# Turned copies of the slots' logits, two separate powers, and later inverses in a decoder block

## The chip, the cores and the metric

The kernel runs on one core of a Trainium2 chip. The metric is the time of one execution on the device in microseconds. Before the change the median of three runs is 528.75 us (527.16 to 528.95).

A core has several engines with instruction queues of their own, which wait for one another by semaphores: TensorE (PE in the profile, its weight loads PEld), VectorE (DVE), ScalarE (ACT), GpSimd (POOL), and SyncE (SP), which issues the DMAs here.

## The reference, cut to what matters

Self-attention, then cross-attention over 64 sequences, then a soft mixture of experts. The change lies in the last part. N is 64 tokens, D 128, 16 experts with 16 slots each (256 slots), and S 128 sequences.

```python
xn = _layernorm(x, ln_gamma, ln_beta)
x_unit = _l2norm(xn, axis=-1)                 # x / max(norm, 1e-12)
mu_unit = _l2norm(mu, axis=0)
logits = jnp.einsum('bnd,des->bnes', x_unit * scale, mu_unit)
dispatch = jax.nn.softmax(logits, axis=1)     # over the tokens
combine = jax.nn.softmax(logits.reshape(B, N, E * S), axis=-1)   # over the slots
slot_in = jnp.einsum('bnd,bnes->besd', xn, dispatch)
h = gelu(jnp.einsum('besd,edh->besh', slot_in, w1) + b1)
slot_out = jnp.einsum('besh,ehd->besd', h, w2) + b2
out = jnp.einsum('besd,bnes->bnd', slot_out, combine)
x = x + out
```

The same logits are wanted twice: with tokens on the partitions (for `dispatch` and its use as a weight), and with slots on the partitions (for `combine`).

## The kernel before

The work is cut into 16 chunks of 512 tokens (8 sequences). Three stages follow each other: self-attention (to about 130 us), cross-attention (to about 300 us), and the experts, in two halves. The first half, called dispatch here (class `Dispatch`, about 300 to 446 us), computes norms, logits, both softmaxes' exponentials, the slots' inputs and the hidden layer before its GELU; the second, combine (class `SecondLayer`, to the end), does GELU, the second matmul, and the sum over slots.

In dispatch all engines walk over steps t = -1 to 15, one chunk a step, in an order that is written out by hand, and each engine works on another chunk: at step t DVE takes the statistics of chunk t+5 (`moments`, `gathered`), the sums of squares of t+3 (`total`), the unit tokens of t+2 (`unit`), and the maxima of t+1 (`maxima`, `negate`). PE at step t computes the slots' logits of chunk t+1 (`logits_T`: 2 matmuls of 512 columns), half of the slots' inputs of chunk t (`gather`), the tokens' logits of t+1 (`logits`: 4 matmuls of 256 columns from the turned unit tokens `xuT` and `mu`), the other half of `gather`, then turns the maxima (`turn_maxima`), turns the unit tokens of t+2 (`turn_tokens`), adds the negated maxima to both sets of logits (`shifts`), and does the first expert layer and the softmax sums of chunk t (L1424, L1432). ACT does the layernorm's scaling (`hat_of`), the squares, the copies out of PSUM and the exponentials. POOL at step t multiplies chunk t+3 with gamma and adds beta (`affine`), scales the hidden layer of chunk t-3 with the inverse softmax sums (L1303), adds the bias (L1307), and computes `roots`: (variance + eps)^-0.5 of chunk t+5 and the inverse norm of chunk t+3 in one power of 8 columns.

The softmax sums travel by DMA: SP sends them to memory (`send_sums`), fetches them in another layout (`fetch_sums`), DVE inverts them (`invert`, tile e_inv), SP sends the inverses (`inverses_out`) and fetches them spread over partitions (`inverses_in`, tile e_rden). All of it stands in SP's queue, one after the other. The last two inverses are sent in `tail_sp` in the first steps of combine; DVE inverts chunk 14 after its last work of dispatch, and chunk 15 after step 2 of combine.

## Time and profile before

| | value |
|---|---|
| median of 3 runs | 528.75 us |
| the profiled execution | 530.01 us |
| its span on the core | 528.1 us |
| PE busy | 479.7 us, 91% |
| DVE busy | 401.5 us, 76% |
| ACT busy | 366.6 us, 69% |
| POOL busy | 291.9 us, 55% |
| granted TensorE clock, mean | 0.989 |

The span lies inside the time of the execution; 1.9 us are around it. A row of a timeline has the start, the length, the engine, the line, the operation, the tiles (out<-in), and in brackets how long the engine was idle before it and what released it. Rows that follow each other on PE overlap a little, since the next matmul enters while the last one drains; the distance of two starts is what the work takes in sequence.

### The profile page before, as it was taken

How to read it: one execution, taken by the hardware profiler on the slowest of the kernel's cores; microseconds unless marked ns; L12 is line 12 of the kernel's file. 1: busy time of each engine (PE TensorE's matmuls, PEld its weight loads, DVE VectorE, ACT ScalarE, POOL GpSimd, SP SyncE). 2: the span in 40 equal slices, each digit the busy share in tenths (PEclk: the TensorE clock that was granted, in tenths of full speed). 3: DMA queues.
4: the chain of work that ended last, by engine and by line, in shares of the span. 5: the costliest groups of instructions: out<-in, count | busy, mean ns of one | idle time of the engine just before them, and what ended most of it. 6: DMA issues, size and time to landing. Idle time of an engine off the chain costs nothing. (4 is left out here: it accounts for less than half of the span.)

```text
span 528.1 us, 21715 instructions
## 1 busy us (share of the span) xinstructions
PE 479.7 (91%) x8732; PEld 325.9 (62%) x8732; DVE 401.5 (76%) x1095; ACT 366.6 (69%) x554; POOL 291.9 (55%) x398
## 2 busy tenths in 40 slices
PE   3999978989779999999997889999999997889996
PEld 2777756655346666666665645656565655668885
DVE  4788568889998898998978666666666544669896
ACT  3888735556678888787887568887889667445550
POOL 4444133555677868787757747798889731111000
PEclk9999989999999999999999989999999999899999
DMA  5377447540000101101111012232322224256554
GB/s 189 87 182 207 121 134 186 145 135 0 3 24 26 44 25 37 35 26 43 26 46 44 3 41 83 83 104 84 107 82 105 83 104 148 80 159 198 187 182 137
DMA packets 53313, 49.32 MB, mean 93 GB/s; under 512 B 14064, under 2 KB 40944, under 8 KB 53232
## 3 DMA queue, kind: packets, MB, share of 16 engines
q1 hardware_dynamic: 53232, 48.20, 30.6%
q8 instruction: 56, 0.92, 0.7%
q14 instruction: 25, 0.20, 0.1%
HBM read 30.87 MB, written 17.04 MB: 91 GB/s over the span
## 5 line engine op out<-in xcount | busy, mean ns | idle before, releaser
L613 DVE TENSOR_REDUCE c_mx<-ps 128x16 f32<-128x1024 f32 x64 | 77.9, 1218 | 12.2 <-PE ps L795 12.1
L553 POOL TENSOR_TENSOR copies_or_layer<-k_or_hidden,w_mask 128x512 bf16<-128x512 f32 x80 | 83.6, 1071 | 1.2 <-DVE c_work L644 1.2
L714 ACT ACTIVATE c_work<-ps 128x2048 f32<-128x2048 f32 x32 | 60.0, 1874 | 27.3 <-PE ps L824 27.3
L1474 ACT ACTIVATE copies_or_layer<-k_or_hidden 32x512 f32 (+1 forms) x64 | 40.2, 628 | 30.9 <-PE ps L1502 30.3
L1349 ACT ACTIVATE e_slot_in<-ps 128x1024 f32<-128x1024 f32 x30 | 30.6, 1019 | 26.0 <-PE ps L1404 26.0
L1303 POOL TENSOR_TENSOR e_scaled<-e_raw,e_rden 128x512 f32<-128x512 f32 x16 | 20.8, 1300 | 45.2 <-DMA e_rden<-dispatch_inverses 45.2
L1487 DVE TENSOR_TENSOR o_slot_out<-ps,w_b 128x512 f32<-128x512 f32 x64 | 40.9, 682 | 5.9 <-PE ps L1502 5.3
L724 ACT ACTIVATE c_q_bd<-x_all,w_mask 128x512 f32<-128x512 f32 x64 | 42.7, 715 | 0.0
L1579 PE MATMUL ps<-o_slot_out,ctx_sb 128*64 128x129 f32 x512 | 37.6, 286 | 4.1 <-DVE o_slot_out L1487 3.7
L1502 PE MATMUL ps<-w_w,copies_or_layer 64*32 64x128 f32 x2048 | 38.1, 277 | 1.2 <-DVE o_slot_out L1487 0.6
L573 POOL COPY c_v_bd<-v_or_front 64x512 f32<-64x512 f32 x32 | 21.8, 682 | 29.8 <-PE ps L844 28.7
L1404 PE MATMUL ps<-copies_or_layer,v_or_front 64*128 64x256 f32 x256 | 36.6, 406 | 0.4 <-ACT copies_or_layer L1371 0.4
L824 PE MATMUL ps<-c_q_bd,k_or_hidden 32*64 32x256 f32 x1024 | 35.7, 375 | 0.9 <-issue 0.9
L1579 PEld LDWEIGHTS ps<-o_slot_out,ctx_sb 128*64 128x64 f32 x512 | 29.9, 139 | 10.4 <-issue 9.8
L844 PE MATMUL ps<-c_work,c_v_bd 128*18 128x64 f32 x2048 | 34.9, 220 | 0.1
L1404 PEld LDWEIGHTS ps<-copies_or_layer,v_or_front 64*128 64x128 f32 x256 | 22.5, 189 | 19.6 <-issue 17.1
L844 PEld LDWEIGHTS ps<-c_work,c_v_bd 128*18 128x18 f32 x2048 | 29.4, 98 | 7.5 <-issue 7.5
L1149 PE MATMUL ps<-v_or_front,w_mu 128*128 128x512 f32 x64 | 32.8, 636 | 1.3 <-ACT v_or_front L1366 1.3
L1502 PEld LDWEIGHTS ps<-w_w,copies_or_layer 64*32 64x32 f32 x2048 | 29.3, 107 | 7.5 <-issue 7.2
L795 PE MATMUL ps<-copies_or_layer,c_q_lead 64*64 64x512 bf16 x256 | 26.4, 399 | 6.5 <-DVE c_mx L613 3.8
L1159 PE MATMUL ps<-w_mu,v_or_front 128*128 128x256 f32 x128 | 31.8, 391 | 0.0
L1262 DVE RECIPROCAL e_inv<-e_sums 128x16 f32<-128x16 f32 x16 | 4.0, 253 | 35.9 <-DMA e_sums<-dispatch_sums 35.9
...
## 6 DMA issues: line engine op xcount, KB each, us to landing
...
```

The source lines that it names most:

```text
L553: ins = nc.gpsimd.tensor_tensor(k_bd[:, c.m2, s, :], k32[:, c.v, :], w["mask8"][:, s:s + 1].to_broadcast([P, TOK]), ALU.mult)
L613: nc.vector.reduce_max(mx[:, c.m2, :, p], ps[:, SCORE:SCORE + 2, :].rearrange("p a (h m) -> p (a h) m", m=N), AX_X).then_inc(mx_sb.sem, 1)
L714: nc.scalar.activation(prob[:, h, :], ps[:, 0:4, :].rearrange("p a b -> p (a b)"), ACT.Exp, scale=float(HD) ** -0.5).then_inc(p_sb.sem, 1)
L724: ins = nc.scalar.activation(q_bd[:, c.m2, j, :], q32[:, c.v, :], ACT.Copy, scale=w["mask4"][:, j:j + 1])
L824: ins = nc.tensor.matmul(ps[N * r:N * (r + 1), T, a * 4 * N:(a + 1) * 4 * N].rearrange("p (j n) -> p j n", j=4), k32[rows, c.v, k_at:k_at ...
L844: ins = nc.tensor.matmul(ps[32 * j:32 * j + 2 * V1, VALUE, to:to + N], v_bd[:, c.m2, 2 * a + u, 4 * T + j, :], prob[:, u, of:of + N], star ...
L1149: ins = self.nc.tensor.matmul(self.ps[:, 3 + h, :], self.w["mu"][:, h * P:(h + 1) * P], self.xuT[:, c.m2, :], start=True, stop=False, skip ...
L1404: ins = nc.tensor.matmul(ps[:, bank + r, a * ES:(a + 1) * ES], xn[at, c.m4, 2 * h + a, :], disp[at, c.m2, 2 * h + a, :], start=True, stop= ...
L1474: ins = self.nc.scalar.activation(self.h_bd[at, c.m2, :, :, e % 2, :].rearrange("p s g k -> p g s k"), self.hidden[at, :, bass.ts(c.v, SC ...
L1487: self.nc.vector.tensor_tensor(self.slot_out[:, c.m2, 4 * u:4 * u + 4, a, 0:D], self.ps[:, 2 * u + a, :].rearrange("p (s d) -> p s d", s=4 ...
L1502: ins = self.nc.tensor.matmul(self.ps[32 * q:32 * (q + 1), 2 * u + a, i * D:(i + 1) * D], self.h_bd[rows:rows + 64, c.m2, (i % 2) * PC + 2 ...
L1579: ins = nc.tensor.matmul(ps[N * r:N * (r + 1), 4 + h, (p % 2) * (D + 1):(p % 2 + 1) * (D + 1)], comb[:, c.m2, a, s * N:(s + 1) * N], slot_ ...
```

## The change

In `logits` PE no longer multiplies the unit tokens with `mu`; DVE copies the slots' logits out of PSUM into a new tile `lT` (`copies`: 2 copies of 512 columns a step), and PE turns that copy, with 8 transposes of 128 columns. The turned unit tokens are copied out of PSUM by DVE (`turned_by_dve`) instead of ACT. On POOL the three small operations of the variance become one, and the power of 8 columns becomes two of 4 (`roots` for chunk t+5, `norms` for chunk t+3), and the bias stands behind them. In DVE's step the statistics stand ahead of `unit`, and `invert` stands between the copies and the maxima, one step later than before. SP sends the sums ahead of the inverses of the chunk before. The inverses of chunks 13, 14 and 15 are sent in six steps of combine instead of two in four, and DVE inverts chunk 14 after step 0 and chunk 15 after step 3 of combine.

```diff
@@ cross_attention, POOL @@
-                dispatch.roots(pool, Chunk(None, 0), None)
-                dispatch.roots(pool, Chunk(None, 1), None)
+                dispatch.roots(pool, Chunk(None, 0))
+                dispatch.roots(pool, Chunk(None, 1))
                 dispatch.affine(pool, Chunk(None, 0))
                 dispatch.affine(pool, Chunk(None, 1))
-                dispatch.roots(pool, Chunk(None, 2), Chunk(None, 0))
-                dispatch.roots(pool, Chunk(None, 3), Chunk(None, 1))
+                dispatch.roots(pool, Chunk(None, 2))
+                dispatch.norms(pool, Chunk(None, 0))
+                dispatch.roots(pool, Chunk(None, 3))
+                dispatch.norms(pool, Chunk(None, 1))
@@ Dispatch @@
-    def roots(self, pool, c, u):
-
-        nc, w, root = self.nc, self.w, self.root
-        both, mv = self.inv_root, self.mv
-        if c:
-            pool.wait_ge(self.stat.sem, self.stat.at(c))
-            if c.plus(-2): pool.wait_ge(self.hat_sb.sem, self.hat_sb.at(c.plus(-2)))
-            v, rc = mv[:, c.m2, :, 1], both[:, c.m2, 1]
-            nc.gpsimd.tensor_tensor(rc, v, w["ln_eps"][:], ALU.add).then_inc(root.sem, 1)
-            pool.wait_ge(root.sem, root.at(c, 1))
-            nc.gpsimd.tensor_tensor(rc, rc, w["ln_eps"][:], ALU.mult).then_inc(root.sem, 1)
-            pool.wait_ge(root.sem, root.at(c, 2))
-            nc.gpsimd.tensor_tensor(rc, rc, v, ALU.add).then_inc(root.sem, 1)
-            pool.wait_ge(root.sem, root.at(c, 3))
-        if u: pool.wait_ge(self.clamped.sem, self.clamped.at(u))
-        if c and u:
-            nc.gpsimd.tensor_tensor(both[:, c.m2], both[:, c.m2], self.halves[:], ALU.pow).then_inc(root.sem, 1)
-            pool.wait_ge(root.sem, root.at(c, 4))
-        elif c:
-            nc.gpsimd.tensor_tensor(both[:, c.m2, 1], both[:, c.m2, 1], self.halves[:, 1], ALU.pow).then_inc(root.sem, 1)
-            pool.wait_ge(root.sem, root.at(c, 4))
-        elif u:
-            nc.gpsimd.tensor_tensor(both[:, u.m2, 0], both[:, u.m2, 0], self.halves[:, 0], ALU.pow).then_inc(self.last_unit, 1)
-        if c:
-            nc.gpsimd.tensor_tensor(self.shift[:, c.m2], mv[:, c.m2, :, 0], both[:, c.m2, 1], ALU.mult).then_inc(root.sem, 1)
-            pool.wait_ge(root.sem, root.at(c, 5))
-            nc.gpsimd.tensor_tensor(self.shift[:, c.m2], self.shift[:, c.m2], self.minus[:], ALU.mult).then_inc(root.sem, 1)
+    def roots(self, pool, c):
+        if not c:
+            return
+        nc, root, mv, rc, shift = self.nc, self.root, self.mv, self.inv_root[:, c.m2, 1], self.shift[:, c.m2]
+        pool.wait_ge(self.stat.sem, self.stat.at(c))
+        if c.plus(-2): pool.wait_ge(self.hat_sb.sem, self.hat_sb.at(c.plus(-2)))
+        nc.gpsimd.tensor_scalar(rc, mv[:, c.m2, :, 1], 1.0 + LN_EPS, LN_EPS ** 2, ALU.mult, ALU.add).then_inc(root.sem, 1)
+        pool.wait_ge(root.sem, root.at(c, 1))
+        nc.gpsimd.tensor_tensor(rc, rc, self.halves[:], ALU.pow).then_inc(root.sem, 1)
+        pool.wait_ge(root.sem, root.at(c, 2))
+        nc.gpsimd.tensor_tensor(shift, mv[:, c.m2, :, 0], rc, ALU.mult).then_inc(root.sem, 1)
+        pool.wait_ge(root.sem, root.at(c, 3))
+        nc.gpsimd.tensor_tensor(shift, shift, self.minus[:], ALU.mult).then_inc(root.sem, 1)
+
+    def norms(self, pool, c):
+        if not c:
+            return
+        pool.wait_ge(self.clamped.sem, self.clamped.at(c))
+        self.nc.gpsimd.tensor_tensor(self.inv_root[:, c.m2, 0], self.inv_root[:, c.m2, 0], self.halves[:], ALU.pow).then_inc(self.inverse.sem, 1)
...
-        if c.plus(2): dve.wait_ge(self.root.sem, self.root.at(c.plus(2), 4))
-        else: dve.wait_ge(self.last_unit, c.v - (CHUNKS - 2) + 1)
+        dve.wait_ge(self.inverse.sem, self.inverse.at(c))
...
+    def copies(self, dve, c):
+        if not c:
+            return
+        if c.plus(-1): dve.wait_ge(self.lA_ps.sem, self.lA_ps.at(c.plus(-1)))
+        for h in range(2):
+            dve.wait_ge(self.lT_ps.sem, self.lT_ps.at(c, h + 1))
+            self.nc.vector.tensor_copy(self.lT[:, h, :], self.ps[:, 3 + h, :]).then_inc(self.lT_sb.sem, 1)
+
+    def turned_by_dve(self, dve, c):
+        if not c:
+            return
+        dve.wait_ge(self.xuT_ps.sem, self.xuT_ps.at(c))
+        if c.plus(-2): dve.wait_ge(self.lT_ps.sem, self.lT_ps.at(c.plus(-2)))
+        self.nc.vector.tensor_copy(self.xuT[:, c.m2], self.ps[:, 0, :]).then_inc(self.xuT_sb.sem, 1)
@@ Dispatch.logits_T, logits @@
-        ins.then_inc(self.lT_ps.sem, 1)
+            ins.then_inc(self.lT_ps.sem, 1)
...
+        pe.wait_ge(self.lT_sb.sem, self.lT_sb.at(c))
         for p in range(PC):
-
-            ins = self.nc.tensor.matmul(self.ps[:, 1 + p // 2, p % 2 * ES:(p % 2 + 1) * ES], self.xuT[:, c.m2, p * P:(p + 1) * P],
-                                        self.w["mu"][:], start=p % 2 == 0, stop=False, skip_group_check=True)
+            for h in range(2):
+
+                at = p % 2 * ES + h * P
+                ins = self.nc.tensor.matmul(self.ps[:, 1 + p // 2, at:at + P], self.lT[:, h, p * P:(p + 1) * P], self.w["ident"][:],
+                                            start=p % 2 == 0 and h == 0, stop=False, is_transpose=True, skip_group_check=True)
@@ Dispatch.rest @@
             if k == 0:
-                inverses_out(sp, end.plus(-1))
+                inverses_out(sp, end.plus(-2))
                 send_sums(sp, end)
             elif k == 1:
-                inverses_in(sp, end.plus(-1))
+                inverses_in(sp, end.plus(-2))
                 fetch_sums(sp, end)
             elif k == 2:
+                inverses_out(sp, end.plus(-1))
+            elif k == 3:
+                inverses_in(sp, end.plus(-1))
+            elif k == 4:
...
+                c = t.plus(0)
+                if c and c.plus(1): send_sums(sp, c)
                 c = t.plus(-1)
-                if c and c.plus(2):
+                if c and c.plus(3):
                     inverses_out(sp, c)
                     inverses_in(sp, c)
                 c = t.plus(0)
-                if c and c.plus(1):
-                    send_sums(sp, c)
-                    fetch_sums(sp, c)
+                if c and c.plus(1): fetch_sums(sp, c)
...
+                self.roots(pool, t.plus(5))
+                self.norms(pool, t.plus(3))
+                if c:
                     pool.wait_ge(divided.sem, divided.at(c))
                     nc.gpsimd.tensor_tensor(hidden[:, :, c.v * QS:(c.v + 1) * QS], scaled[:, c.m2],
                                             w["b1"][:].rearrange("p (g o) -> p g o", o=1).to_broadcast([P, 4, QS]),
                                             ALU.add).then_inc(biased.sem, 1)
-                self.roots(pool, t.plus(5), t.plus(3))
...
+                    self.moments(dve, t.plus(5))
                     self.unit(dve, t.plus(2))
-                    self.moments(dve, t.plus(5))
+                    self.copies(dve, t.plus(1))
+                    c = t.plus(-2)
+                    if c and c.plus(3): invert(dve, c)
                     self.maxima(dve, t.plus(1))
                     self.gathered(dve, t.plus(5))
                     self.negate(dve, t.plus(1))
                 self.total(dve, t.plus(3))
-                c = t.plus(-1)
-                if c and c.plus(2): invert(dve, c)
+                self.turned_by_dve(dve, t.plus(2))
...
-            invert(dve, end.plus(-1))
+            invert(dve, end.plus(-2))
...
-                self.turned(act, t.plus(2))
@@ SecondLayer.rest, DVE @@
-                if t.i is None and t.k == 2: dispatch.invert(dve, Chunk(None, CHUNKS - 1))
+                if t.i is None and t.k == 0: dispatch.invert(dve, Chunk(None, CHUNKS - 2))
+                if t.i is None and t.k == 3: dispatch.invert(dve, Chunk(None, CHUNKS - 1))
```

One step of DVE's queue in the middle of dispatch, before (e_stats statistics, e_cm and e_rm maxima, e_ss sums of squares, L1092 the unit tokens):

```order
L1092 TENSOR_TENSOR v_or_front<-v_or_front,e_inv_root 128x512
L1051 BN_STATS e_stats<-x_all 128x6 x4
L1101 TENSOR_REDUCE e_cm<-ps 128x16
L1105 TENSOR_REDUCE e_rm<-ps 128x2 x2
L1062 BN_AGGR e_mv<-e_stats 128x2 x4
L1113 TENSOR_SCALAR e_neg<-ps 128x256
L1081 TENSOR_REDUCE e_ss<-v_or_front 128x4
L1084 TENSOR_SCALAR e_inv_root<-e_ss 128x4
L1262 RECIPROCAL e_inv<-e_sums 128x16
```

The same step after:

```order
L1049 BN_STATS e_stats<-x_all 128x6 x4
L1089 TENSOR_TENSOR v_or_front<-v_or_front,e_inv_root 128x512
L1098 COPY e_lT<-ps 128x512 x2
L1281 RECIPROCAL e_inv<-e_sums 128x16
L1113 TENSOR_REDUCE e_cm<-ps 128x16
L1117 TENSOR_REDUCE e_rm<-ps 128x2 x2
L1060 BN_AGGR e_mv<-e_stats 128x2 x4
L1125 TENSOR_SCALAR e_neg<-ps 128x256
L1079 TENSOR_REDUCE e_ss<-v_or_front 128x4
L1082 TENSOR_SCALAR e_inv_root<-e_ss 128x4
L1105 COPY v_or_front<-ps 128x512
```

Three copies out of PSUM are added (L1098 twice, L1105), the statistics stand ahead of the unit tokens, and the inverse of the sums stands behind the copies.

One step of POOL's queue in the middle of dispatch, before (e_halves is the power of -0.5, w_gamma and w_beta the affine part, L1303 and L1307 the hidden layer of an earlier chunk):

```order
L1009 TENSOR_TENSOR e_inv_root<-e_mv,w_ln_eps 128x4
L1011 TENSOR_TENSOR e_inv_root<-e_inv_root,w_ln_eps 128x4
L1013 TENSOR_TENSOR e_inv_root<-e_inv_root,e_mv 128x4
L1017 TENSOR_TENSOR e_inv_root<-e_inv_root,e_halves 128x8
L1025 TENSOR_TENSOR e_shift<-e_mv,e_inv_root 128x4
L1027 TENSOR_TENSOR e_shift<-e_shift,e_minus 128x4
L997 TENSOR_TENSOR v_or_front<-v_or_front,w_gamma 128x512
L999 TENSOR_TENSOR v_or_front<-v_or_front,w_beta 128x512
L1303 TENSOR_TENSOR e_scaled<-e_raw,e_rden 128x512
L1307 TENSOR_TENSOR k_or_hidden<-e_scaled,w_b 128x4x128
```

The same step after:

```order
L1001 TENSOR_TENSOR v_or_front<-v_or_front,w_gamma 128x512
L1003 TENSOR_TENSOR v_or_front<-v_or_front,w_beta 128x512
L1322 TENSOR_TENSOR e_scaled<-e_raw,e_rden 128x512
L1013 TENSOR_SCALAR e_inv_root<-e_mv 128x4
L1015 TENSOR_TENSOR e_inv_root<-e_inv_root,e_halves 128x4
L1017 TENSOR_TENSOR e_shift<-e_mv,e_inv_root 128x4
L1019 TENSOR_TENSOR e_shift<-e_shift,e_minus 128x4
L1025 TENSOR_TENSOR e_inv_root<-e_inv_root,e_halves 128x4
L1329 TENSOR_TENSOR k_or_hidden<-e_scaled,w_b 128x4x128
```

The bias of the hidden layer (L1329) now stands right behind the power that gives the inverse norms (L1025).

DVE's queue from the last maxima of dispatch into combine, before (L1335 the last slots' inputs, o_slot_out the second layer's output with its bias):

```order
L1105 TENSOR_REDUCE e_rm<-ps 128x2 x2
L1113 TENSOR_SCALAR e_neg<-ps 128x256
L1262 RECIPROCAL e_inv<-e_sums 128x16
L1329 COPY e_raw<-ps 128x1024
L1480 MEMSET o_slot_out 128x32
L1335 COPY e_slot_in<-ps 128x2x2x256 x2
L1487 TENSOR_TENSOR o_slot_out<-ps,w_b 128x4x128 x4
L1262 RECIPROCAL e_inv<-e_sums 128x16
L1537 UNCONDITIONAL_BRANCH
L1487 TENSOR_TENSOR o_slot_out<-ps,w_b 128x4x128 x2
L1544 RECIPROCAL o_rden<-ps 128x2
L1548 SCALAR_TENSOR_TENSOR o_y<-ps,o_rden,x_all 128x128 x2
```

The same place after:

```order
L1117 TENSOR_REDUCE e_rm<-ps 128x2 x2
L1125 TENSOR_SCALAR e_neg<-ps 128x256
L1352 COPY e_raw<-ps 128x1024
L1502 MEMSET o_slot_out 128x32
L1358 COPY e_slot_in<-ps 128x2x2x256 x2
L1509 TENSOR_TENSOR o_slot_out<-ps,w_b 128x4x128 x4
L1281 RECIPROCAL e_inv<-e_sums 128x16
L1559 UNCONDITIONAL_BRANCH
L1509 TENSOR_TENSOR o_slot_out<-ps,w_b 128x4x128 x2
L1566 RECIPROCAL o_rden<-ps 128x2
L1570 SCALAR_TENSOR_TENSOR o_y<-ps,o_rden,x_all 128x128 x2
L1509 TENSOR_TENSOR o_slot_out<-ps,w_b 128x4x128 x2
```

No inverse stands ahead of L1352 any more; the one behind L1509 is that of chunk 13 instead of chunk 14.

## Rows read from the trace of the kernel before

**Rows 1.** Busy times by stretch: busy (instructions) PE PEld DVE ACT POOL, PEclk, DMA, GB/s.

```profile
130.00:300.00 170.00, 155.53 (x3948) 102.30 (x3947) 147.21 (x263) 133.13 (x175) 126.82 (x154) 1.00 0.11 30
360.00:390.00 30.00, 30.00 (x348) 17.51 (x350) 18.87 (x56) 25.80 (x39) 26.62 (x35) 1.00 0.30 101
```

**Rows 2.** Timeline of PE, one step: start us, length us, engine, line, what [idle before <-releaser].

```profile
370.30 1.98 PE L1149 MATMUL ps<-v_or_front,w_mu 128*128 128x512 f32 x4
...
373.28 1.99 PE L1159 MATMUL ps<-w_mu,v_or_front 128*128 128x256 f32 x8
375.20 1.13 PE L1404 MATMUL ps<-copies_or_layer,v_or_front 64*128 64x256 f32 x8
376.34 0.22 PE L1174 MATMUL ps<-e_ident,e_cm 128*8 128x128 bf16 x2
...
376.55 0.66 PE L1186 MATMUL ps<-w_ident,v_or_front 128*128 128x128 f32 x4
...
379.10 1.98 PE L1149 MATMUL ps<-v_or_front,w_mu 128*128 128x512 f32 x4
```

**Rows 3.** Timeline of DVE, the same step.

```profile
371.95 1.24 DVE L1092 TENSOR_TENSOR v_or_front<-v_or_front,e_inv_root 128x512 f32<-128x512 f32 x1
373.11 0.86 DVE L1051 BATCH_NORM_STATS2 e_stats<-x_all 128x6 f32<-128x128 f32 x4
373.89 1.20 DVE L1101 TENSOR_REDUCE e_cm<-ps 128x16 bf16<-128x1024 f32 x1
375.01 1.27 DVE L1105 TENSOR_REDUCE e_rm<-ps 128x2 bf16<-128x512 f32 x2
376.21 0.36 DVE L1062 BATCH_NORM_AGGREGATE e_mv<-e_stats 128x2 f32<-128x6 f32 x4
376.68 0.43 DVE L1113 TENSOR_SCALAR e_neg<-ps 128x256 bf16<-128x256 f32 x1
```

**Rows 4.** Timeline of POOL, the same step, and a power of four columns later.

```profile
371.36 1.27 POOL L997 TENSOR_TENSOR v_or_front<-v_or_front,w_gamma 128x512 f32<-128x512 f32 x1
...
375.62 1.04 POOL L1307 TENSOR_TENSOR k_or_hidden<-e_scaled,w_b 128x512 f32<-128x512 f32 x1
376.65 0.20 POOL L1009 TENSOR_TENSOR e_inv_root<-e_mv,w_ln_eps 128x4 f32<-128x4 f32 x1
376.93 0.20 POOL L1011 TENSOR_TENSOR e_inv_root<-e_inv_root,w_ln_eps 128x4 f32<-128x4 f32 x1
...
412.99 1.02 POOL L1023 TENSOR_TENSOR e_inv_root<-e_inv_root,e_halves 128x4 f32<-128x4 f32 x1 [1.26 <-DVE e_inv_root L1084]
```

**Rows 5.** Timeline of PE: where dispatch begins, and its last slots' logits.

```profile
299.92 1.89 PE L1159 MATMUL ps<-w_mu,v_or_front 128*128 128x256 f32 x8
...
307.34 3.04 PE L1149 MATMUL ps<-v_or_front,w_mu 128*128 128x512 f32 x4 [1.34 <-ACT v_or_front L1366]
...
431.68 1.98 PE L1149 MATMUL ps<-v_or_front,w_mu 128*128 128x512 f32 x4
```

**Rows 6.** Timeline of DVE where dispatch begins.

```profile
300.85 0.68 DVE L1092 TENSOR_TENSOR v_or_front<-v_or_front,e_inv_root 128x512 f32<-128x512 f32 x1
```

**Rows 7.** Timeline of DVE, end of dispatch and start of combine.

```profile
441.55 0.25 DVE L1262 RECIPROCAL e_inv<-e_sums 128x16 f32<-128x16 f32 x1 [3.14 <-DMA e_sums<-dispatch_sums]
441.72 1.16 DVE L1329 COPY e_raw<-ps 128x1024 f32<-128x1024 f32 x1
...
453.53 0.25 DVE L1262 RECIPROCAL e_inv<-e_sums 128x16 f32<-128x16 f32 x1 [3.18 <-DMA e_sums<-dispatch_sums]
...
470.81 0.25 DVE L1262 RECIPROCAL e_inv<-e_sums 128x16 f32<-128x16 f32 x1 [2.93 <-DMA e_sums<-dispatch_sums]
```

**Rows 8.** Timeline of PE, end of dispatch and start of combine.

```profile
445.21 1.08 PE L1424 MATMUL ps<-e_slot_in,w_w 128*32 128x128 f32 x32 [2.31 <-DVE e_slot_in L1335]
...
455.07 2.01 PE L1579 MATMUL ps<-o_slot_out,ctx_sb 128*64 128x129 f32 x16 [1.66 <-DVE o_slot_out L1487]
...
472.34 1.15 PE L1579 MATMUL ps<-o_slot_out,ctx_sb 128*64 128x129 f32 x16 [2.04 <-DVE o_slot_out L1487]
```

16 lines of the change are left out of this document (9 added, 7 removed).

## The prediction

> **What bounds the kernel now.** I read the busy times by stretch first, to see which engine never rests in dispatch, where nearly all edits lie. In the middle of dispatch PE is busy 30.00 us of 30.00 at granted clock 1.00, with DVE at 18.87, ACT at 25.80 and POOL at 26.62 [rows 1]. The timeline of PE then gives the step: from one pair of slots' logits (L1149) to the next 8.80 us, without idle time [rows 2]. From chunk 1 to chunk 15 the same instruction moves from 307.34 to 431.68, 124.34 us in 14 steps, of which the first is long because its matmuls start slowly (3.04 instead of 1.98 us) [rows 2, 5]; the rest are 8.77 each. The chain of waits names the DMAs of the sums and inverses for this stretch, but PE's own row has no gap, so I take that chain as level with PE, not ahead of it. The waits that PE does have stand behind dispatch: DVE waits 3.14, 3.18 and 2.93 us for sums [rows 7], and PE behind it 2.31, 1.66 and 2.04 us [rows 8].
>
> **PE's step after.** Four matmuls of 256 columns leave, whose start lies 1.92 us before the next instruction's (373.28 to 375.20) [rows 2]. Eight transposes of 128 columns come; four of the same kind (L1186) take 0.66 us with the drain of the last, which is 0.07 for L1159 (1.99 against 1.92), so eight are 2 x 0.66 less 0.1, or 1.22 [rows 2]. PE alone would have a step of 8.77 - 0.70 = 8.07 us.
>
> **The wait that is added.** The transposes wait for DVE's copies of L1149's result. A copy out of PSUM of 1024 columns takes 1.16 us [rows 7], so one of 512 is about 0.60. If DVE is free, the second starts when L1149 is through, 1.98 + 0.04 us into the step, and ends at 2.62; PE is ready for the transposes at 2.98 (373.28 - 370.30) [rows 2]. Behind it on DVE stand the inverse (0.17, 441.55 to 441.72) [rows 7], the column maxima (1.12) and the row maxima (1.20 to 1.27) [rows 3], so the maxima end at 5.2; PE needs them after its own 2.98 + 1.22 + 1.06 = 5.26. From the turned maxima to the next L1149 are 2.76 us (376.34 to 379.10) [rows 2]. With DVE free the loop is 8.0 to 8.1, just covered by PE.
>
> **Is DVE free? The loop through POOL.** I think not, in 8 of the 14 steps. The unit tokens (L1092 before) stand ahead of the copies and wait for the inverse norms. In one before-row this instruction took 1.24 us instead of its usual 0.68 [rows 3, 6]: it started at 371.95 while POOL's multiplication of 512 columns ran from 371.36 to 372.63, and it ended at 373.19, 0.56 behind it [rows 4]. So the two exclude each other, and who comes first holds the other off. Now the bias (1.04) stands right behind the power, on POOL itself, and POOL's next instruction enters without a gap (375.62 + 1.04 against 376.65) [rows 4], while DVE has to hear a semaphore. I expect POOL to win and the unit tokens to wait for the bias. The loop is then, in us: signal that the statistics are there 0.1; the variance 0.28 (376.65 to 376.93); power of four columns 1.02 + 0.07; two shifts 0.28 + 0.15; second power 1.0; bias 1.0 [rows 4]; unit tokens behind it 0.56; two copies 1.20; inverse 0.17; column maxima 1.12; row maxima 1.20; statistics gathered 0.36 [rows 3]. That is 8.51 us, 0.26 under 8.77. It holds where POOL has both statistics ahead (to step 10) and a bias behind (from step 3): 8 steps. The other 6 go at PE's 8.1, 0.67 less each. The bounds: with the DVE first, all steps 8.1; if the added copies too were held off by POOL's multiplications, 0.5 more, 9.0. I take 8.51, since a held off instruction is in the rows and a held off copy isn't.
>
> The Trainium skill (GPSIMD Engine Reference, Specifications) says that VectorE and GpSimd contend for SBUF where the DVE instruction has two SBUF inputs or a two-port mode. By that rule the unit tokens contend and copies out of PSUM don't; the trace agrees on the first. By it the step would be 8.5, not 9.0.
>
> Sum in dispatch: 8 x 0.26 + 6 x 0.67 = 6.1, and 0.6 for the transposes of chunk 15 behind the last of these steps: **6.7 us gained**.
>
> **Other edits of POOL and ACT.** POOL drops two operations of 0.28 with their gaps and pays 1.02 + 1.02 for powers where it paid one; both are inside the loop above or beside PE. The copy that ACT loses was beside PE; on DVE it stands last in the step, about 0.5 us before L1149 wants it (maxima negated, sums 0.88, copy 0.6, against 2.76 - 0.34 on PE), so nothing.
>
> **SP.** The sums now go ahead of the inverses, and DVE's inverse of a chunk comes a step later; behind it SP needs about 1.6 (landing) + 1.8 (four issues) + 2 to 3 (sums back) = 5.4 to 6.4 us, less than a step of 8.1. Cost nothing; if the landings were slow together it would be some tenths in a few steps.
>
> **Where dispatch begins.** Before, PE did the first tokens' logits at 299.92 [rows 5]. Now the copies stand behind DVE's unit tokens, which start at 300.85 [rows 6]; two copies end at about 302.7, and cross-attention's last turns on PE are queued behind them. The maxima come 1.2 us later, the first negation 1.6, and then the turned tokens' copy waits on DVE behind sums and the last residual: L1149 at about 309.2 instead of 307.34 [rows 5]. **Loss 1.9**; between 1.2 (only the maxima's delay) and 3.0 (if the slow matmuls grow as well).
>
> **End of dispatch and combine.** (a) The inverse that waited 3.14 us to 441.55 stood ahead of the copies of the last slots' inputs [rows 7]; with it gone the copy of e_raw (1.16) runs about 1 us sooner, right behind PE's sums, and L1424 can start at about 444.3 instead of 445.21 [rows 8]: 0.9. (b) The inverse of chunk 14 at 453.53, with 3.18 us of waiting, held up o_slot_out, and PE's L1579 at 455.07 [rows 7, 8]; chunk 13 stands there now, whose sums were fetched a step before. Of the 3.18 PE had other work for about 0.9, so L1579 could start about 452.8: 2.3. It then ran 2.01 us instead of 1.15 [rows 8], and slower matmuls followed; of about 1.4 so lost I count 0.8. (c) The inverse of chunk 15 at 470.81 waited 2.93 and held PE 2.04 us [rows 7, 8]. One step of combine (4.4 us) later the sums are there: 2.0. Together **6.0 gained**; between 3.5, if one of the waits only moves, and 7.0. What is late next is PE itself, which has work without gaps in combine.
>
> **Sum.** 6.7 - 1.9 + 6.0 = 10.8 us. The profiled execution took 530.01 (span 528.1 and 1.9 around it), so 519.2. It lay 1.3 above the median of the runs; for the median I predict 528.75 - 10.8 = **518.0 us**.
>
> **Rivals.** *PE's step in full*: DVE gets in ahead of the bias, all 14 steps are 8.1. For it: no row shows this pair released by one instruction; against it: POOL's entry without a gap, above. Gain 14 x 0.67 - 6.1 = 3.3 more: 514.7 us. *The step stays at 8.77*: the chain of DMAs that the profile names, or DVE with three more copies, holds the old pace. For it: the chain's view; against it: SP has one wait less per turn. 518.0 + 6.7 = 524.7. *Copies held off too*: steps of 9.0, 14 x 0.23 = 3.2 lost where 6.1 were gained: 518.0 + 9.3 = 527.3. *Slower*: the small gaps on PE make the granted clock fall inside dispatch. A step of 8.1 at the low level (1.2 instead of 2.4 GHz) is at most 16.2; from two such steps on (+16) the kernel is slower: 534. For it: L1149 at 307.34 and L1579 at 455.07 ran slowly right behind idle times of 1.34 and 1.66 us [rows 5, 8]. Against it: cross-attention idles 14.5 of 170 us and has clock 1.00 [rows 1], and the gaps here are 0.2 to 0.3 us.
> The Trainium skill (TensorE: Matmul & The Clock Gate, Part 4: PE-mode transpose) says that transposes don't count as busy in the way that matmuls do, which speaks for this last rival, since 12 of them stand in a step instead of 4; no row here shows that many.
>
> **Chances.** Forecast 0.42; PE in full 0.25; step unchanged 0.15; copies held off 0.10; slower 0.08. A change of under 0.5% (2.6 us) could hardly be told from none. Forecast, full step and unchanged step lie below 526.1: faster 0.82; the held off copies are the same: 0.10; slower 0.08. The likeliest case alone reaches from 515.5 to 520.5 (start 1.1 worse, end 2.5 worse or 1.0 better, clock). The range for 8 in 10 takes in the full step, with its own spread, and the unchanged one: 512.5 to 525.5.
>
> **What would show it.** In the trace after: L1149's successor from chunk to chunk every 8.5 us in steps 3 to 10 and 8.1 elsewhere; the unit tokens at 1.5 us, starting with the bias on POOL; short waits of PE for the copy and the row maxima; eight transposes in 1.2 us; no wait of DVE for sums in combine. The forecast is wrong in its step if the unit tokens take 0.6 us and PE has no gaps, or if DVE waits for sums in dispatch; in its sign if the granted clock in dispatch is under 0.95.

## The result, and the profile after

| | before | after |
|---|---|---|
| median of the runs | 527.95 us (526.86 to 528.95, 4 runs) | 522.0 us (519.15 to 525.64, 4 runs) |
| the profiled execution | 530.01 us | 521.1 us |
| its span | 528.1 us | 519.3 us |
| PE busy | 479.7 us, 91% | 464.6 us, 89% |
| DVE busy | 401.5 us, 76% | 436.1 us, 84% |
| ACT busy | 366.6 us, 69% | 360.2 us, 69% |
| POOL busy | 291.9 us, 55% | 289.4 us, 56% |
| granted TensorE clock, mean | 0.989 | 0.993 |

The ratio is 0.9889, with an interval of 0.9846 to 0.9933: the change makes the kernel about 1.1% faster. Repeated beside the experiments, the changed kernel gave 0.9882 [0.9857, 0.9907], with a median of 523.54 us.

Four landmarks on PE cut the two profiles into pieces that can be compared: the start of the slots' logits of chunks 0, 1 and 15 (L1149 before, L1161 after), and the end of PE's last matmul.

| us | before | after | gained |
|---|---|---|---|
| to chunk 0's slots' logits | 297.66 | 296.54 | 1.12 |
| chunk 0 to chunk 1 | 9.68 | 12.52 | -2.84 |
| chunk 1 to chunk 15, 14 steps | 124.34 | 117.41 | 6.93 |
| chunk 15 to PE's end | 92.00 | 88.13 | 3.87 |
| PE's end to the end of the span | 4.42 | 4.70 | -0.28 |

The pieces add up to the 8.8 us between the spans. The 1.12 us of the first row lie ahead of dispatch, where only POOL's small operations differ; over all the profiles of this case this landmark lies between 296.54 and 299.62, so I don't count them as the change's.

This is PE in a step in the middle of dispatch of the changed kernel. It answers to [rows 2] (start, length, engine, line, what, and in brackets the idle time before and what ended it).

```profile
360.03 1.99 PE L1161 MATMUL ps<-v_or_front,w_mu 128*128 128x512 f32 x4
...
363.31 1.07 PE L1174 MATMUL ps<-w_ident,e_lT 128*128 128x128 f32 x8 [0.23 <-DVE e_lT L1098]
364.30 1.13 PE L1426 MATMUL ps<-copies_or_layer,v_or_front 64*128 64x256 f32 x8
365.64 0.22 PE L1189 MATMUL ps<-e_ident,e_cm 128*8 128x128 bf16 x2 [0.20 <-DVE e_rm L1117]
...
368.40 1.99 PE L1161 MATMUL ps<-v_or_front,w_mu 128*128 128x512 f32 x4
```

The step is 8.37 us (360.03 to 368.40). PE now has two short waits in it, for the copy and for the row maxima, and the eight transposes take 0.99 us (363.31 to 364.30). DVE in the same step, for [rows 3]:

```profile
365.51 0.36 DVE L1060 BATCH_NORM_AGGREGATE e_mv<-e_stats 128x2 f32<-128x6 f32 x4
...
368.81 1.52 DVE L1089 TENSOR_TENSOR v_or_front<-v_or_front,e_inv_root 128x512 f32<-128x512 f32 x1 [0.23 <-POOL e_inv_root L1025]
370.25 1.28 DVE L1098 COPY e_lT<-ps 128x512 f32<-128x512 f32 x2
371.45 0.24 DVE L1281 RECIPROCAL e_inv<-e_sums 128x16 f32<-128x16 f32 x1
371.61 1.16 DVE L1113 TENSOR_REDUCE e_cm<-ps 128x16 bf16<-128x1024 f32 x1
```

And POOL, for [rows 4]:

```profile
365.96 0.19 POOL L1013 TENSOR_SCALAR e_inv_root<-e_mv 128x4 f32<-128x4 f32 x1 [0.30 <-DVE e_mv L1060]
366.24 1.02 POOL L1015 TENSOR_TENSOR e_inv_root<-e_inv_root,e_halves 128x4 f32<-128x4 f32 x1
...
367.77 1.01 POOL L1025 TENSOR_TENSOR e_inv_root<-e_inv_root,e_halves 128x4 f32<-128x4 f32 x1
368.74 1.04 POOL L1329 TENSOR_TENSOR k_or_hidden<-e_scaled,w_b 128x512 f32<-128x512 f32 x1
369.74 1.72 POOL L1001 TENSOR_TENSOR v_or_front<-v_or_front,w_gamma 128x512 f32<-128x512 f32 x1
```

The power frees both engines; the bias enters POOL at 368.74, the unit tokens enter DVE at 368.81 and end at 370.33, 0.55 behind the bias, where alone they take 0.68. The next POOL operation then takes 1.72 instead of 1.27. The copies that follow on DVE take their normal 1.28 for two, although POOL is still in L1001. The whole forecast loop can be walked in these rows: statistics at 365.87, POOL at 365.96, bias at 368.74, unit tokens until 370.33, maxima from 371.61, and the next statistics gathered 8.37 later. POOL waits 0.30 for them: it is a ring in which each engine waits a little for the others.

Where dispatch begins, PE and DVE of the changed kernel, for [rows 5, 6]:

```profile
296.54 1.98 PE L1161 MATMUL ps<-v_or_front,w_mu 128*128 128x512 f32 x4
...
301.67 1.97 PE L1174 MATMUL ps<-w_ident,e_lT 128*128 128x128 f32 x8 [2.71 <-DVE e_lT L1098]
...
309.06 1.12 PE L1161 MATMUL ps<-v_or_front,w_mu 128*128 128x512 f32 x2 [1.58 <-DVE v_or_front L1105]
```

```profile
299.73 0.68 DVE L1089 TENSOR_TENSOR v_or_front<-v_or_front,e_inv_root 128x512 f32<-128x512 f32 x1
300.32 1.28 DVE L1098 COPY e_lT<-ps 128x512 f32<-128x512 f32 x2
```

PE idles 2.71 us until the copies are there, the same eight transposes then take 1.97 (the granted clock is 1.00 from 296.5 to 301.5 and 0.66 in the five us behind it), and the next chunk's logits wait 1.58 for the turned tokens' copy, which DVE does now. The end of dispatch and combine, on PE, for [rows 8]:

```profile
438.65 1.08 PE L1446 MATMUL ps<-e_slot_in,w_w 128*32 128x128 f32 x32 [1.59 <-DVE e_slot_in L1358]
...
443.41 1.29 PE L1524 MATMUL ps<-w_w,copies_or_layer 64*32 64x128 f32 x70 [1.33 <-issue]
...
459.33 0.91 PE L1524 MATMUL ps<-w_w,copies_or_layer 64*32 64x128 f32 x45 [0.89 <-issue]
463.28 1.11 PE L1602 MATMUL ps<-o_slot_out,ctx_sb 128*64 128x129 f32 x15 [0.61 <-issue]
```

For [rows 7], DVE's inverses have no idle time any more:

```profile
445.09 0.24 DVE L1281 RECIPROCAL e_inv<-e_sums 128x16 f32<-128x16 f32 x1
...
465.16 0.24 DVE L1281 RECIPROCAL e_inv<-e_sums 128x16 f32<-128x16 f32 x1
```

So all waits for sums are gone, and where they were, PE now stops for "issue", for nothing that the profile shows. From 8 us behind the last slots' logits on, PE's waits for semaphores fell from 7.02 to 2.61 us, and its issue stops rose from 0.95 to 3.39.

### The profile page after: what moved, and what is told of

Read it like the earlier page. It is cut to its first block, busy times and chain, and to the rows that moved or that the text cites. A ratio compares the mean times of both kernels' runs of the same rounds, so it can differ in the third digit from the quotient of the medians.

```text
span 519.3 us, 21727 instructions
## 1 busy us (share of the span) xinstructions
PE 464.6 (89%) x8732; PEld 316.3 (61%) x8732; DVE 436.1 (84%) x1142; ACT 360.2 (69%) x539; POOL 289.4 (56%) x380
## 4 chain that ended last, share of the span: by engine, by line
PE 40%; DVE 34%; issue 11%; POOL 7%; ACT 5%; DMA 2%; DVEq 0%; SPq 0%; POOLq 0%; ACTq 0%
DVE c_mx L615 11%; PE ps L1602 7%; PE ps L1524 7%; PE ps L826 4%; DVE c_work L646 3%; DVE copies_or_layer L606 3%; PE ps L923 3%; PE ps L1161 3%; PE ps L797 3%; DVE e_lT L1098 3%; DVE e_cm L1113 3%; PE ps L366 2%; PE ps L859 2%; POOL c_rstd L563 2%; PE ps L375 2%
## 5 line engine op out<-in xcount | busy, mean ns | idle before, releaser
L1509 DVE TENSOR_TENSOR o_slot_out<-ps,w_b 128x512 f32<-128x512 f32 x64 | 41.2, 685 | 8.3 <-PE ps L1524 8.0
L1161 PE MATMUL ps<-v_or_front,w_mu 128*128 128x512 f32 x64 | 31.7, 618 | 1.6 <-DVE v_or_front L1105 1.6
L646 DVE TENSOR_SCALAR c_work<-x_all,c_mv,c_rstd 128x128 f32<-128x128 f32 x64 | 24.2, 439 | 6.7 <-POOL c_rstd L563 6.7
L606 DVE TENSOR_SCALAR copies_or_layer<-k_or_hidden,w_mask 128x512 bf16<-128x512 f32 x48 | 29.4, 612 | 0.0
```

What stands on the lines that cost most here:

```text
L606: ins = nc.vector.tensor_scalar(k_bd[:, c.m2, s, :], k32[:, c.v, :], w["mask8"][:, s:s + 1], None, ALU.mult)
L1161: ins = self.nc.tensor.matmul(self.ps[:, 3 + h, :], self.w["mu"][:, h * P:(h + 1) * P], self.xuT[:, c.m2, :], start=True, stop=False, skip ...
```

## The experiments

The stretches named in all of them are those of the table above. Ratios are to the kernel before, on the same chip.

### The changed kernel again

> The changed kernel itself, to be compared on one chip with the next three. Both theories: ratio to before between 0.984 and 0.993, step 8.37 us in the middle of dispatch.

Measured: 523.54 us, 0.9882 [0.9857, 0.9907]. The 14 steps are 117.40 us (117.41 in the first profile). The other stretches are not as steady: 11.23 from chunk 0 to chunk 1 (12.52), where PE idles the same 2.71 us but the granted clock stays at 1.00 and the eight transposes take 1.09 instead of 1.97, and 90.58 from chunk 15 to the end (88.13). The latter has 4.03 us of issue stops (3.39), and one of them has a consequence. PE in the repeated run:

```profile
463.37 1.11 PE L1602 MATMUL ps<-o_slot_out,ctx_sb 128*64 128x129 f32 x15 [1.98 <-issue]
464.41 1.89 PE L1524 MATMUL ps<-w_w,copies_or_layer 64*32 64x128 f32 x64
466.23 1.96 PE L1602 MATMUL ps<-o_slot_out,ctx_sb 128*64 128x129 f32 x16
468.12 1.16 PE L1524 MATMUL ps<-w_w,copies_or_layer 64*32 64x128 f32 x64
```

Busy times by stretch over these instructions (busy and count of PE, PEld, DVE, ACT, POOL, then the granted clock, DMA share and GB/s), of the repeated run and then of the first profile of the changed kernel:

```profile
463.30:467.30 4.00, 3.93 (x89) 3.38 (x91) 1.76 (x6) 0.61 (x1) 0.00 (x0) 0.66 0.39 127
```

```profile
463.30:467.30 4.00, 4.00 (x154) 3.46 (x159) 2.90 (x9) 1.87 (x3) 0.00 (x0) 1.00 0.54 165
```

Behind a stop of 1.98 us the granted clock was 0.66 and PE did 89 instructions in 4 us; behind a stop of 0.61 it was 1.00 and PE did 154. The length of a stop doesn't decide this alone: stops of 1.71 and 1.72 us at the same place in three other kernels (unit tokens first, chunk 0 as before, turned tokens on ACT) were followed by a clock of 1.00. The kernel's spread over its runs (519.15 to 525.64) has room for such differences from run to run.

### Who goes first, the bias or the unit tokens

```diff
                     pool.wait_ge(divided.sem, divided.at(c))
+                    if t.plus(3): pool.wait_ge(self.xu_sb.sem, self.xu_sb.at(t.plus(3)))
                     nc.gpsimd.tensor_tensor(hidden[:, :, c.v * QS:(c.v + 1) * QS], ...
```

> The changed kernel, with one more wait on POOL: the bias of the hidden layer waits until DVE has done the unit tokens that the power just released. Theory A (the step of 8.37 us runs through POOL: bias and unit tokens exclude each other, POOL comes first, and the copies for the transposes wait behind the unit tokens): the unit tokens fall from 1.52 to about 0.65 us, PE's waits for the copy and the row maxima (0.23 and 0.21) vanish or nearly so, the step in the middle of dispatch falls to 7.9 to 8.2 us, and the kernel is 2 to 4 us faster than the changed one (ratio to before about 0.983). Rival B (POOL's own work is as long as the step, so what DVE gains POOL loses): POOL's wait for the statistics (0.30) vanishes, the step stays at 8.3 to 8.4 and the time within 0.5 us.

Measured: 526.84 us, 0.9923 [0.9892, 0.9953]. The middle step grew to 8.62, the 14 steps to 118.94. POOL, DVE and PE in that kernel:

```profile
371.34 1.04 POOL L1330 TENSOR_TENSOR k_or_hidden<-e_scaled,w_b 128x512 f32<-128x512 f32 x1 [0.87 <-DVE v_or_front L1089]
```

```profile
370.50 0.69 DVE L1089 TENSOR_TENSOR v_or_front<-v_or_front,e_inv_root 128x512 f32<-128x512 f32 x1 [1.21 <-POOL e_inv_root L1025]
```

```profile
367.96 1.08 PE L1447 MATMUL ps<-e_slot_in,w_w 128*32 128x128 f32 x32 [0.46 <-ACT e_slot_in L1373]
```

The unit tokens are short again (0.69), which confirms that the bias was what held them. But POOL now idles 0.87 us a step and has 7.75 of work, which is the 8.62; its product with beta ends later, ACT's square waits for it (1.30), ACT's copy of the slots' inputs stands behind the square, and PE waits for that. Theory A fell: taking the exclusion off DVE doesn't bring 8.1, because POOL has no room for the wait. Rival B named the right engine, but had the step stay at 8.3 to 8.4, and it grew. The exclusion costs DVE 0.84 us a step (1.52 against 0.68) or POOL 0.87, and the order decides which. The times can't show the 0.25 us a step, since the intervals of this kernel and of the changed kernel's repetition overlap; the steps in the profile do.

### Statistics gathered ahead of the unit tokens

```diff
                     self.moments(dve, t.plus(5))
+                    self.gathered(dve, t.plus(5))
                     self.unit(dve, t.plus(2))
@@
                     self.maxima(dve, t.plus(1))
-                    self.gathered(dve, t.plus(5))
                     self.negate(dve, t.plus(1))
```

> The changed kernel, with DVE's gathering of the statistics right behind the statistics themselves instead of behind the row maxima. Theory A' (the step is a loop: statistics gathered, POOL's two powers and the bias, unit tokens, copies, maxima, statistics gathered; PE, DVE and POOL each have slack in it): POOL's wait of 0.30 us for the statistics vanishes, and the step falls from 8.37 to 8.0 to 8.2 us in the middle of dispatch, in all 1.5 to 2.5 us less than the changed kernel. Rival B (POOL's own work of 8.1 us, or the squares that wait for it on ACT, is next at once): the step falls by less than 0.15 us, or PE then waits for ACT's slot copies as it did where the bias waited for the unit tokens.

Measured: 520.6 us, 0.9849 [0.9818, 0.9879]; the 14 steps are 114.16, 3.2 us less, where 1.5 to 2.5 were expected. The time's interval overlaps the repetition's, so the gain is shown by the steps. POOL, DVE and PE in a middle step:

```profile
364.66 0.19 POOL L1013 TENSOR_SCALAR e_inv_root<-e_mv 128x4 f32<-128x4 f32 x1
...
367.44 1.04 POOL L1329 TENSOR_TENSOR k_or_hidden<-e_scaled,w_b 128x512 f32<-128x512 f32 x1
```

```profile
367.65 0.38 DVE L1060 BATCH_NORM_AGGREGATE e_mv<-e_stats 128x2 f32<-128x6 f32 x4
367.95 1.08 DVE L1089 TENSOR_TENSOR v_or_front<-v_or_front,e_inv_root 128x512 f32<-128x512 f32 x1
368.95 1.27 DVE L1098 COPY e_lT<-ps 128x512 f32<-128x512 f32 x2
```

```profile
362.33 1.09 PE L1174 MATMUL ps<-w_ident,e_lT 128*128 128x128 f32 x8
363.61 1.13 PE L1426 MATMUL ps<-copies_or_layer,v_or_front 64*128 64x256 f32 x8 [0.19 <-ACT e_slot_in L1372]
```

POOL no longer waits for statistics: those that it takes at 364.66 were gathered one step (8.12) ahead of 367.65 and ready at 359.9. The steps are 8.12. That is not PE's work alone: in each middle step PE waits 0.19 us for ACT's copy of the first half of the slots' inputs, which must be done before the second half starts, so its own work is about 7.93. That copy (1.02 us) and its semaphores now have to fit beside transposes of 1.09 us, where matmuls of 1.99 stood. The exclusion is still there (0.55 behind the bias: 369.03 against 368.48), and it no longer sets the step. This is the test that shows the loop to be the bound of the changed kernel's 8.37.

### The tokens' logits by matmul again

```diff
 copies:
+        return
 logits:
-        pe.wait_ge(self.lT_sb.sem, self.lT_sb.at(c))
         for p in range(PC):
-            for h in range(2): ... self.lT[:, h, p * P:(p + 1) * P], self.w["ident"][:], ... is_transpose=True
+            ins = self.nc.tensor.matmul(..., self.xuT[:, c.m2, p * P:(p + 1) * P], self.w["mu"][:], ...)
```

The copy of the turned tokens waits for these matmuls, which read the tile that it overwrites.

> The changed kernel with the tokens' logits as matmuls with mu in all chunks, without DVE's two copies; all other edits stay. Theory A (only the transposes shorten dispatch, since PE had no idle time in it): PE is without gaps again, the step is 8.77 us, the 14 steps take about 123 instead of 117.4 us, the start is about 2.8 us shorter, and the kernel is 2 to 4 us slower than the changed one and still 3 to 5 faster than before by its end. Rival B (the new order on DVE, POOL and SP shortens the step): the step is under 8.6 us.

Measured: 528.0 us, 0.996 [0.9933, 0.9987]; 124.26 for the 14 steps, 8.77 each. Its busy times in dispatch:

```profile
345.00:375.00 30.00, 30.00 (x312) 17.91 (x311) 24.04 (x55) 24.53 (x37) 26.87 (x31) 1.00 0.28 95
```

PE is back at 30.00 of 30.00: all the gain in the 14 steps comes from the turned copies, and the other edits of dispatch alone give none of it. They don't lose any either while PE is the bound. The whole kernel's ratio is that of the later inverses alone, further down (0.996 and 0.9963). Behind dispatch its issue stops are 4.20 us, but at other instructions than in the changed kernel: at x16 and x2 of a group, as before the change, and at x37 and x8. Counted in PE's matmuls from chunk 15's slots' logits, the stops of this kernel stand at 414, 668, 793 and 918, and those of the changed kernel at 280, 660, 785 and 911. A stop belongs to a place in the stream of PE's instructions; with other instructions in dispatch the places lie 7 or 8 matmuls elsewhere.

### Chunk 0's logits as before

```diff
 copies:
+        if not c.plus(-1): return
 logits:
+        if not c.plus(-1):
+            for p in range(PC): ... matmul(..., self.xuT[:, c.m2, p * P:(p + 1) * P], self.w["mu"][:], ...)
+            return
```

The copy of the turned tokens of chunk 2 waits for these matmuls, which read the tile that it overwrites.

> The changed kernel, but the tokens' logits of chunk 0 come from the matmuls with mu as before; all other chunks turn the copy. Theory A (the start of dispatch lost 2.8 us because PE waits 2.71 us for DVE's copies of chunk 0, and its queue behind them holds up cross-attention's last turns): the distance from the slots' logits of chunk 0 to those of chunk 1 falls from 12.5 us to about 10, and the kernel is 2 to 3 us faster than the changed one. Rival B (what is late there is DVE, which now also copies the turned tokens before PE may go on): the distance falls by less than 1 us.

Measured: 522.67 us, 0.986 [0.9818, 0.9902]. From chunk 0 to chunk 1 PE takes 9.91 instead of 12.52 (11.23 in the repeated run), so the loss at the start is the added copies' and sits where it was expected. Of the 2.6 us against the first profile, 1.3 are the low clock behind the idle time, which the repeated run didn't have. The time can't confirm either: the interval overlaps the changed kernel's own.

### Both edits of dispatch together

The two diffs above (statistics, chunk 0) in one kernel.

> The changed kernel with both repairs: the statistics gathered early, and chunk 0's logits as before. If both give what they give alone: slots' logits of chunk 0 to chunk 1 in 9.9 us instead of 12.5, steps of 8.0 to 8.2, so 4 to 5 us less than the changed kernel (ratio to before about 0.980). Rival B: only the start is gained, 2 to 2.6 us.

Measured: 520.29 us, 0.9819 [0.9798, 0.984], against 0.9882 [0.9857, 0.9907] of the changed kernel in the same comparison. Chunk 0 to chunk 1 takes 9.92 and the 14 steps 115.36, whose first is 9.76 where it was 8.56. That is the clock and not the edit: this profile has 0.66 from 309 to 314, with the slots' logits of chunk 1 at 3.36 us instead of 1.98, and the kernel above, with the same edit and the same wait of 1.58 us before them, has 1.00 there and a first step of 8.56. This version beats both kernels; its interval lies wholly below the changed kernel's.

### Inverses later still

```diff
-            if k == 0: inverses_out(sp, end.plus(-2)); send_sums(sp, end)
-            elif k == 1: inverses_in(sp, end.plus(-2)); fetch_sums(sp, end)
-            ... k == 2 to 5: the other inverses
+            if k == 0: send_sums(sp, end)
+            elif k == 1: fetch_sums(sp, end)
+            ... k == 4 to 9: the inverses of chunks 13, 14, 15
```

> The changed kernel, with the inverses of chunks 13, 14 and 15 sent in steps 4 to 9 of combine instead of 0 to 5, and DVE's inverse of chunk 15 after step 6. In the changed kernel PE stops for 0.89 and 0.61 us at 458.5 and 462.7 with no semaphore as the cause, while the DMA engines are 55% busy. Theory A (PE's instructions arrive by DMA, and those of the loop's first turn come late because the transfers of the inverses fill the DMA engines): the two stops fall under 0.3 us together, 1 to 1.5 us gained. Rival B (the stops belong to the first turn of PE's loop whatever the DMAs do): they stay, and the time too.

Measured: 523.74 us, 0.9859 [0.9811, 0.9907]. Three issue stops of 1.61, 1.02 and 1.45 us stayed. The one of 0.89 us of the changed kernel (x45 of a group) is absent, and that of 0.61 is the one of 1.45 here: neither theory's number, and no gain in the sum. The last of them on PE:

```profile
466.28 1.11 PE L1596 MATMUL ps<-o_slot_out,ctx_sb 128*64 128x129 f32 x15 [1.45 <-issue]
```

At 466.28 none of the inverses had been sent yet (the first goes out at 474.04 in SP's queue). So the stops don't come from the transfers that the change moved. They stand at the same instructions as in the changed kernel (x70, x10 and x15 of a group), and so do those of its variants at full traffic.

### Later inverses alone

The last two inverses, of chunks 14 and 15, sent and made later (SP's steps and DVE's places in combine) in the kernel before, all else as before.

> The kernel before, with its last two inverses alone moved: DVE inverts chunk 14 after step 0 and chunk 15 after step 3 of combine, and SP sends them in steps 1 to 5. Theory A (what the waits for the sums cost is what their removal gives): from the first expert layer of chunk 15 to the last matmul 4.5 to 5.5 us less than the 76.5 of before, and the kernel 1% faster. Rival B (PE's instructions arrive late in combine's first steps, and the waits covered it): PE's waits for DVE go, stops without a semaphore of 3 to 4 us in sum take their place, and 2 to 3 us are gained, 0.5%.

Measured: 527.6 us, 0.9963 [0.9945, 0.9981]. In the profile PE's waits for semaphores behind dispatch fell from 7.02 to 2.59 us, as in the changed kernel, but the issue stops grew from 0.95 to 2.28; chunk 15 to the end takes 88.08 instead of 92.00. The profile shows 3.9 us and the runs 2.0 (0.37% of 529.6, between 1.0 and 2.9): one profile has one draw of the stops, and this one has no stretch at the low clock behind dispatch, as the kernel before has one (455 to 458). From the landmark that the expectation names, L1424 of chunk 15, to the end it is 78.47 before (not 76.5) and 75.27 here. So Theory A's 4.5 us aren't reached; Rival B is nearer: its gain of 2 to 3 us is met at its lower end, but its stops of 3 to 4 us in sum are 2.28.

### Less traffic in combine

```diff
+        if c.i is None and 2 <= c.k < 8:
+            sp.dma_start(self.comb[0:2, c.m2]..., comb_dram[bass.ds(c.v, 1), 0:2]...)
+            return
@@
+                    if t.i is None and t.k < 6:
+                        sp.dma_start(out_v[bass.ds(c.v, 1), a, 0:2]..., y[N * a:N * a + 2, c.m2])...
```

> The changed kernel with most of two kinds of transfers cut to two rows each: the loads of the context of chunks 2 to 7, and the stores of the output in combine steps 0 to 5; that part of the output is left out. Theory A: the stops of TensorE that the profile names issue (about 3.4 to 5.1 us in the stretch from the slots' logits of chunk 15 to the end, over the kernels run so far) come from these transfers standing in the way of TensorE's instructions; then they fall under 1 us in that stretch, and the stretch, 88.1 to 90.6 us so far, takes 85 to 86. Rival B: the stops are tied to places in TensorE's instruction stream and not to the data's transfers; they stay between 2.5 and 5 us, the stretch within 88 to 90.6, and the time within 0.5% of the changed kernel's 522 to 523.5.

Measured: 520.57 us, 0.981 [0.9752, 0.9867], which overlaps the changed kernel's interval; chunk 15 to the end 86.68. Of the issue stops on PE that the view shows in that stretch, these two are left:

```profile
445.81 1.29 PE L1528 MATMUL ps<-w_w,copies_or_layer 64*32 64x128 f32 x70 [1.34 <-issue]
...
513.55 2.01 PE L1609 MATMUL ps<-o_slot_out,ctx_sb 128*64 128x129 f32 x32 [0.36 <-issue]
```

The three stops between 450 and 470 us are gone from it (1.70 us in the changed kernel, 3.04 in its repetition); the first of them is still there with 0.12 us, under the 0.15 that the view shows. The one at 445.81 remains: ahead of it stand transfers that were not cut (DMA share 0.87 from 436.88 to 442.88). That they cause it wasn't tried. The 0.36 is in every kernel, before too. So neither theory is met in full: the stops are 1.70 us in sum where A had under 1, and the stretch lies between the two forecasts. A is right for three of the four stops, and B, which tied them to their places alone, is wrong on these, though right that each place is fixed. The page of the changed kernel shows a DMA queue of the instructions themselves, on the same 16 engines as the data:

```profile
q8 instruction: 56, 0.92, 0.7%
```

That is 56 packets, 0.92 MB, or 16,384 bytes each. In the kernel with less traffic they start 3.6 to 3.8 us apart from 450.8 to 461.9; in the repetition of the changed kernel at 450.5, 455.8 and 461.0, 5.2 us apart, and PE's stop of 1.98 ended at 463.37. No view names the engine that this queue feeds, but the times of its packets do nearly as much. In the twelve profiles PE has 43 issue stops over 0.15 us behind the start of dispatch, the one of 0.36 apart, and each of them ends 1.1 to 1.6 us after the end of the last packet. Their places lie 125 to 127 matmuls apart, or twice that, and 126 matmuls take about 3.4 us in combine (80 in 2.17), nearly the distance of the packets. So PE is fed in blocks of its instructions, a packet each, and stops where a block ends and the next isn't there. That data beside a block delays it is shown by this one kernel and profile. It isn't the whole cause: in the kernel with the logits as matmuls the stop of 0.78 us at 452.99 had a DMA share of 0.04 from 446.5 until its packet at 450.2, and of 0.84 only before that, from 442 to 446.5.

### The turned tokens' copy on ACT again

```diff
 DVE:
-                self.turned_by_dve(dve, t.plus(2))
 ACT:
                 if t.plus(1): slots(t.plus(0), 1)
+                self.turned(act, t.plus(2))
```

> The changed kernel with the turned unit tokens copied from PSUM by ScalarE instead of VectorE, as before the change; everything else as changed. Theory A: the loop that sets the step runs over POOL's statistics, powers and bias and over VectorE's unit tokens, and the copies of the turned tokens lie behind it whichever engine does them; the step of the 14 stays within 0.1 us of 8.37, and the time within 0.5% of the changed kernel's. Rival B: VectorE's 0.6 us a step less lets its maxima and gathered sums start earlier; the step falls to about 8.1 and the time by 2 to 4 us. Rival C: ScalarE's copy stands behind its exponentials and slot copies, TensorE waits for it before the slots' logits; the step grows by 0.2 to 0.4 us and the time by 3 to 6 us.

Measured: 525.12 us, 0.9899 [0.9867, 0.9931]; middle step 8.37, 14 steps 117.75. Theory A holds, on the step and within 0.5% on the time. DVE lost 0.6 us of work and idles for it:

```profile
368.94 1.52 DVE L1089 TENSOR_TENSOR v_or_front<-v_or_front,e_inv_root 128x512 f32<-128x512 f32 x1 [0.83 <-POOL e_inv_root L1025]
```

The wait for the power grew from 0.23 to 0.83 us. The loop goes round that copy, and which engine does it doesn't matter here.

## Why the prediction came out as it did

The sign and the loop in dispatch were right; the change gave 8.9 us in the profiles, 1.1 of them ahead of dispatch, against the 10.8 forecast, and the medians 6 us (527.95 to 522.0). The forecast of 518.0 was 4.0 too low. The measured 522.0 lies in the range of 512.5 to 525.5 by the range's breadth, and outside the 515.5 to 520.5 given for the likeliest case. The gain fell short by 4.8 us; that the number is off by only 4.0 comes from the kernel before, whose median moved from 528.75 to 527.95 with a fourth run.

**PE's step.** The transposes were put at 1.22 us and took 0.99: 0.125 each without idle time. PE alone was put at 8.07. The shortest steps are 8.12 (the last two, and nearly all with early statistics), which looks like a hit and is luck: PE's own work is about 7.93, and the rest is the wait of 0.19 us for ACT's copy of the slots' inputs, which the prediction didn't have among its waits.

**The loop through POOL.** Named with all its members and confirmed by three runs: early statistics break it, putting the unit tokens first moves it to POOL, and an unloaded DVE doesn't touch it. It was put at 8.51 and is 8.37 in the eight middle steps; walked in the rows, no term is off by more than 0.08. The unit tokens end 0.55 us behind the bias, as taken from [rows 3, 4], and the copies out of PSUM are not held off. By the contention rule of the Trainium skill (GPSIMD Engine Reference, Specifications) quoted in the prediction, that is how the two should differ, and here the trace agrees: 1.28 us for two copies beside POOL, 1.52 against 0.68 for one instruction with two SBUF inputs.

**The other six steps.** "The other 6 go at PE's 8.1" was wrong for four. Without a bias, POOL's next operation, the product with gamma, stands behind the power and holds the unit tokens just as well, and longer. DVE and POOL in the second step:

```profile
318.02 1.75 DVE L1089 TENSOR_TENSOR v_or_front<-v_or_front,e_inv_root 128x512 f32<-128x512 f32 x1 [0.22 <-POOL e_inv_root L1025]
```

```profile
317.96 1.27 POOL L1001 TENSOR_TENSOR v_or_front<-v_or_front,w_gamma 128x512 f32<-128x512 f32 x1
```

These four steps are 8.49 to 8.60. The forecast made the 14 steps 8 x 8.51 + 6 x 8.1 = 116.7 us, and they are 117.4. That 6.93 us were gained where 6.1 were forecast is due to the first step of before: it was 10.37, with the slow matmuls of [rows 5], and the sum had counted it as 8.77. Of the 6.93, 1.6 come from there and 5.3 from the steps as the forecast meant them.

**The start.** Put at 1.9 lost (1.2 to 3.0), measured 2.84 in one profile and 1.55 in the other. Both have PE idle 2.71 us; the first has the transposes at half speed behind it and comes close to the upper bound. With chunk 0's logits as before the loss is 0.23.

**The clock.** The rival in which small gaps pull the granted clock down in dispatch did not happen: waits of 0.2 us, with 12 transposes a step, stayed at a granted clock of 1.00 in both profiles of the changed kernel behind chunk 0's logits (104.28 us of work in 110 us from 318 to 428 in the first). The page of the Trainium skill that was cited for it (TensorE: Matmul & The Clock Gate, Part 4: PE-mode transpose) spoke for such a fall; the measurement decides against it here.

**The end and combine: the step that failed.** The terms (a) 0.9, (b) 2.3 + 0.8 and (c) 2.0, with 0.6 for the last transposes, make 6.6 us from chunk 15 to the end. Measured: 3.87 in the first profile and 1.42 in the repetition; over the seven profiled kernels that have the turned logits and these inverses at full traffic (the changed one, its repetition, unit tokens first, chunk 0 as before, early statistics, both, turned tokens on ACT) the stretch is 88.13 to 90.58, on average 89.6, which is 2.4 gained.

The waits went, as said, but by 4.4 us (7.02 to 2.61), where (a), (b) and (c) without the clock make 5.2. (b) claimed 2.3 for a wait that was 1.66 on PE's own row, and in (a) the wait of 2.31 fell to 1.59 and not away. The sentence that failed is "What is late next is PE itself, which has work without gaps in combine". What came next was the supply of PE's instructions: 3.4 to 5.1 us of issue stops in these seven kernels, 4.4 on average, instead of 0.95. Of that, 0.6 to 1.6 us are a stop right behind dispatch (x70 of a group) that only the kernels with turned logits have, so it comes with the transposes and not with the inverses; the others stand in combine's first steps, where the waits for sums had been. The 0.8 us booked for the low clock did come in six of the seven; in the repetition the low clock came back behind the stop of 1.98.

With the traffic cut, the stretch is 86.68, a gain of 5.3: most of the sum is reachable, but not with these transfers beside it. The missing 4.2 us (6.6 less 2.4) are most of the 4.8 by which the gain fell short: 3.5 of issue stops and 0.8 of waits put too high, about. The other pieces nearly cancel (0.8 more than forecast in the 14 steps, less at the start and behind PE's end). Issue stops stood in the trace of before too, at the same kind of place (0.38 us at 452.95, 0.21 at 463.22). That the longer waits beside them gave the blocks time to arrive fits the three kernels with the logits as matmuls: before, there is no stop over 0.1 us at places 793 and 918; without the waits for sums there are 0.34 and 1.95 in one, and 0.85 at 918 in the other. I read the rows of the waits and not those of the issue stops.
